# Sixty-five transposes of the identity in four of TensorE's waits, in a decoder of two layers on one core

## The chip, the cores and the metric

The kernel runs on one core of a Trainium2 chip. The core has five engines that run their own instruction streams and meet at semaphores: TensorE (matmuls and transposes; PE in the profile, its weight loads PEld), VectorE (DVE), ScalarE (ACT), GpSimd (POOL) and SyncE (SP, here used only to start transfers). TensorE reads from the on-chip memory and writes to eight accumulation banks; the other engines copy results out of these. The metric is the device time of one execution in microseconds, median over runs; lower is better.

## The reference

Two decoder layers in post-norm form over 16 sequences of 64 tokens with 128 features (1,024 tokens, eight tiles of 128). Each layer adds self-attention, cross-attention and a feed-forward part, with a layer norm behind each:

```
x = _layernorm(x + _L0_attn_ref(x, ...))
x = _layernorm(x + _L0_xattn_ref(x, ctx_1024, ctx_1024, mask, ...))
x = _layernorm(x + _L0_ffn_ref(x, gate_w, wg, wu, wd))
x = _layernorm(x + _L1_attn_ref(x, W_qkv, W_out))
x = _layernorm(x + _L1_xattn_ref(x, ctx_1024, ctx_1024, mask, ...))
x = _layernorm(x + _L1_ffn_ref(x, W_fc, ln_w, ln_b, W_proj))
```

The third line is a mixture of experts: a gate picks two of eight experts for each token, each expert computes `silu(x @ wg.T) * (x @ wu.T)` with 512 inner features and projects back with `wd`, and the two results are added with softmax weights. The fourth is self-attention with 16 heads of 64 features ("wide" in the kernel). The last has ternary weights: a matrix is divided by the mean of its magnitudes and rounded to -1, 0 or 1. All inputs and outputs are fp32.

## The kernel before

Each engine's instruction stream is written out by hand, in program order, with semaphore waits; no planner reorders anything. The kernel has three stages.

**First stage.** `stream_pe` and its four companions run the first two attentions as a software pipeline over 16 tiles. `drain_pe` ends it: beside the last tiles it computes the gate's logits, ranks the tokens by expert, and transposes the 24 expert weight matrices in four banks (L1347), each group copied back by ScalarE (L1352). GpSimd scatters the tokens' rows to a table in device memory, in the order of their experts (L1437).

**Experts** (`Routed`). The table is worked off in 23 blocks of 128 rows. For block j TensorE transposes its rows (`block_pe`, L1521, bank 6), ScalarE copies them out (L1527), TensorE does the gate and up projections (L1549, L1557; four matmuls each, which the profile shows as eight, since an fp32 matmul runs in two passes), ScalarE does the SiLU, VectorE the product, TensorE the down projection (L1580, bank 7). `Routed.pe` runs two blocks ahead with the transposes. Transposing block j+1 waits until ScalarE has copied block j out. Before block 0's copy ScalarE has two copies of weights for blocks 0 and 1 in its stream (`bring_act`, L1531); for later blocks GpSimd makes these copies (L1537).

**Bridge and second stage.** Behind the last block TensorE transposes weights of the next layers (L793, L270), multiplies the wide value weights with the output weights (L805), projects a bias (`fc.project_bias`, L985), and makes the column means of the ternary projection (`fc.means_pe`, L1004), for which it waits until VectorE has scaled the projection (L993). GpSimd gathers each token's two expert rows from the table (L1706): tiles 0 and 1, then tile 0's rsqrt (L1729), tile 2, tile 1's rsqrt, tiles 3 and 4, the rsqrt of tiles 2 and 3 (L1727, L1729), and so on in pairs. VectorE combines the rows of a tile (L1714, L1717), takes the statistics, and normalizes (`apply`, L1734). `turn_pe` (L1744) transposes the normalized tile for the next stage, and ScalarE copies it (L1750). Then `stream_pe` starts over with the wide attention: four projections of queries and keys per tile (`qkw_pe`, L831, 32 matmuls in the profile), scores (L858), value projections (L844). Their results go through three banks, 6, 7 and 4, in turn, and ScalarE and VectorE copy them out (L881). VectorE's row maxima are L403.

Bank 4 (`B_Y`) is not used from the end of the first stage to a matmul of two columns at block 8 (L949), and from there to the wide projections. `ident` is the 128 x 128 identity, loaded with the constants at the start.

Of the kernel before, what the change touches and what calls it, by code (L numbers as in the profile page):

```python
# [15 lines left out]
P = 128  # L16
# [62 lines left out]
def decoder_kernel(nc, A, out):  # L79
    with ExitStack() as ctx:  # L80
# [28 lines left out]
        PS = ctx.enter_context(nc.psum_tensor("banks", [P, 8, BANK], F32))  # L109

        B_S, B_PT, B_Y, B_OX, B_K, B_Q = 0, 2, 4, 5, 6, 7
# [74 lines left out]
        ident = cst[:, C_ID:C_ID + P]  # L186
# [65 lines left out]
        class Transposes:  # L252
# [7 lines left out]
            def pe(self, pe, some=None):  # L260
                for g in some or range(len(self.groups)):
                    waits, blocks, _ = self.groups[g]
                    for s, v in waits:
                        pe.wait_ge(s, v)
                    last = g - len(self.banks)
                    if last >= 0:
                        pe.wait_ge(self.copied[last % 2], last // 2 + 1)
                    bank = self.banks[g % len(self.banks)]
                    for n, (src, k) in enumerate(blocks):
                        m = pe.transpose(PS[:, bank, n * P:n * P + k], src, ident[0:k, 0:k])  # L270
                    m.then_inc(self.mm, 1)
# [72 lines left out]
        class Stage:  # L344
# [16 lines left out]
            def x_pe(self, pe, job):  # L361

                i = job.i
                pe.wait_ge(*self.norm.ln.at(i + 1))
                if i + 1 < NT:
                    pe.wait_ge(*self.norm.r.at(i + 2))
                elif job.after is not None and not self.wide and not job.after.stage.early:
                    pe.wait_ge(*job.after.stage.norm.r.at(1))
                if i >= 1:
                    pe.wait_ge(*self.norm.xev.at(i))  # L370
                pe.transpose(PS[:, B_OX, 2 * P:3 * P], X[:, i, :], ident).then_inc(self.norm.xmm.sem, 1)
# [49 lines left out]
            def t_pe(self, pe, job):  # L421

                i, n = job.i, job.n
                pe.wait_ge(*(self.share if self.wide else self.exp).at(i + 1))
                for m in range(2):
                    if job.before:
                        pe.wait_ge(*job.before.pt_read(m))
                    for r in range(4 * m, 4 * m + 4):
                        t = pe.transpose(PS[:, B_PT + m, P * (r % 4):P * (r % 4 + 1)], PR[:, n % 2, P * r:P * (r + 1)], ident)  # L429
                    t.then_inc(self.t_mm.sem, 1)  # L430
# [881 lines left out]
        class Routed:  # L1312
# [183 lines left out]
            def rows_sp(self, sp):  # L1496
# [14 lines left out]
                for j in range(BLOCKS):  # L1511
# [2 lines left out]
                    sp.wait_ge(*self.ycp.at(j + 1))  # L1514
                    sp.dma_start(routed[bass.ds(at[j], P), :], YS[:, j % 3, :]).then_inc(s_ys[j % 3], 16)

            def block_pe(self, pe, j):
                pe.wait_ge(s_xg[j % 4], 16 * (j // 4 + 1))
                if j >= 1:
                    pe.wait_ge(*self.xgt.at(j))  # L1520
                pe.transpose(PS[:, 6, 0:P], XG[:, j % 4, :], ident).then_inc(self.xt_mm.sem, 1)  # L1521
# [69 lines left out]
            def pe(self, pe):  # L1591
                last = pre[-1]
                pe.wait_ge(*last.y_read())
                pe.wait_ge(*self.rk.at(len(GROUPS)))
                pe.wait_ge(*self.map.at(8))
                _, e = nc.values_load_multi_w_load_instructions(
                    bi[0:1, 0, 0:BLOCKS], engines=[mybir.EngineType.PE], min_val=0, max_val=EXPERTS - 1,
                    skip_runtime_bounds_check_because="a sum of seven comparisons, each 0 or 1")
                pe.wait_ge(*self.w_cp.at(3 * EXPERTS))
                self.block_pe(pe, 0)  # L1600
                self.block_pe(pe, 1)
                for n in range(BLOCKS + 1):
                    if n + 2 < BLOCKS:
                        self.block_pe(pe, n + 2)
                    if n == 8:
                        fc.totals(pe, self.mul.at(n - 1))
                    if n < BLOCKS:
                        self.gate_pe(pe, n)
                    if n == 9:
                        pe.wait_ge(*fc.thr.at(2))  # L1610
                    if n < BLOCKS:
                        self.up_pe(pe, n)
                    if n >= 1:
                        self.down_pe(pe, n - 1, e[n - 1])
                pe.wait_ge(s_sep, 3)
                pe.wait_ge(*self.silu.at(BLOCKS))
                wide.weights_pe(pe)
                pe.wait_ge(*self.xgt.at(BLOCKS))
                fct.pe(pe, [0])
                pe.wait_ge(*self.ycp.at(BLOCKS))  # L1620
                fct.pe(pe, [1])
                pe.wait_ge(*self.mul.at(BLOCKS))
                wide.products_pe(pe)
                fc.project_bias(pe)
                fc.means_pe(pe)
                pe.wait_ge(*fc.bias.at(1))
                self.turn_pe(pe, (0,))

# [443 lines left out]
```

## Time and profile before

| | |
|---|---|
| median of three runs | 376.67 us |
| the runs | 373.87, 376.67, 377.61 us |
| profiled execution, first to last instruction | 377.6 us |
| TensorE busy | 336.8 us, 89% of the span |
| VectorE, ScalarE, GpSimd busy | 236.4, 183.6, 202.1 us |
| TensorE's mean granted clock | 0.964 of full speed |

The profiled execution's own time is its span, 377.6 us; it is the same as the highest run to the digit given. Busy time is the time in which an engine has an instruction of its own under way; TensorE's matmuls overlap one another, and their ends are modelled. The granted clock is the share of TensorE's full clock (2.4 GHz) that it was given; in this trace it has two levels, 1.00 and 0.50.

### The profile page before, as it was taken

What the parts mean: (1) busy time and instruction counts of PE and PEld (TensorE: products, weight loads), DVE (VectorE), ACT (ScalarE), POOL (GpSimd) and SP (SyncE); (2) the same over time, 40 slices, a digit from 0 to 9 for tenths busy, and PEclk for the clock granted to TensorE, in tenths of its full rate; (3) what the DMA queues carried; (4) which work ended last, traced back from release to release, by engine and by line L of the source; (5) the groups of instructions that cost most, each with busy time, mean ns of one, the idle gap of its engine ahead of it and who ended that gap; (6) DMA issues with size and microseconds to landing.
All of it is one profiled execution on the core that took longest, in us unless ns stands there. A gap on an engine that the chain in (4) does not pass through costs nothing.

```text
span 377.6 us, 9893 instructions
## 1 busy us (share of the span) xinstructions
PE 336.8 (89%) x3774; PEld 264.6 (70%) x3774; DVE 236.4 (63%) x561; ACT 183.6 (49%) x383; POOL 202.1 (54%) x287
## 2 busy tenths in 40 slices
PE   3879999998885589999997799889999999999994
PEld 2556677665774489999997675657788665676773
DVE  2798987778755013574335477746666577887585
ACT  2466776665653823233224134433544344776641
POOL 1856988885667124553413776322222057476785
PEclk9989999999989669999999699999999999999999
DMA  6799996000001101111101111000000000000001
GB/s 191 219 308 256 293 338 176 2 3 2 30 28 51 43 16 49 50 43 50 44 27 33 36 36 30 2 0 2 2 2 3 3 0 3 2 2 2 3 21 36
DMA packets 35993, 22.98 MB, mean 61 GB/s; under 512 B 4196, under 2 KB 33900, under 8 KB 35820
## 3 DMA queue, kind: packets, MB, share of 16 engines
q1 hardware_dynamic: 34636, 19.64, 17.9%
q0 software_dynamic: 1024, 2.10, 1.9%
q8 instruction: 31, 0.51, 0.5%
q10 hardware_dynamic: 288, 0.62, 0.5%
q14 instruction: 14, 0.11, 0.1%
HBM read 14.61 MB, written 7.73 MB: 59 GB/s over the span
## 4 chain that ended last, share of the span: by engine, by line
PE 76%; DVE 11%; issue 5%; ACT 3%; POOL 2%; DMA 1%; another core or an unknown queue 1%; SPq 0%; POOLq 0%; ACTq 0%; DVEq 0%
PE banks L429 7%; PE banks L844 7%; PE banks L831 6%; PE banks L1549 6%; PE banks L1557 6%; PE banks L539 6%; PE banks L566 6%; PE banks L1580 6%; PE banks L875 3%; PE banks L1347 3%; PE banks L511 3%; PE banks L523 2%; PE banks L1032 2%; PE banks L586 2%; PE banks L582 2%
## 5 line engine op out<-in xcount | busy, mean ns | idle before, releaser
L690 POOL TENSOR_TENSOR KB<-KT,cst 128x512 f32<-128x512 f32 x48 | 49.3, 1048 | 8.2 <-DVE KT L650 6.0
L403 DVE TENSOR_REDUCE mx<-banks 128x16 f32<-128x1024 f32 x32 | 38.6, 1207 | 13.5 <-PE banks L550 11.7
L438 ACT ACTIVATE PT<-banks 128x512 f32<-128x512 f32 x64 | 34.9, 595 | 23.6 <-PE banks L429 22.3
L1572 DVE TENSOR_TENSOR PT<-banks,PR 128x512 f32<-128x512 f32 x23 | 15.9, 691 | 47.9 <-PE banks L1557 43.7
L1537 POOL COPY U<-WALL 128x1024 f32 x21 | 21.9, 1043 | 42.6 <-PE banks L1557 35.9
L881 ACT ACTIVATE U<-banks 128x512 f32<-128x512 f32 x40 | 23.9, 597 | 38.1 <-PE banks L844 22.5
L331 POOL TENSOR_SCALAR ve<-mv 128x1 f32<-128x1 f32 x40 | 9.1, 229 | 54.0 <-DVE mv L326 53.6
L429 PE MATMUL banks<-cst,PR 128*128 128x128 f32 x256 | 35.6, 283 | 0.5 <-POOL PR L910 0.5
L419 ACT ACTIVATE PR<-PR 128x1024 f32<-128x1024 f32 x32 | 33.8, 1058 | 3.4 <-DVE PR L413 3.4
L831 PE MATMUL banks<-XT,WQKV 128*128 128x128 f32 x256 | 33.2, 292 | 0.4 <-ACT XT L1750 0.4
L844 PE MATMUL banks<-WALL,XT 128*64 128x512 f32 x128 | 29.7, 600 | 3.1 <-DVE U L881 2.8
L831 PEld LDWEIGHTS banks<-XT,WQKV 128*128 128x128 f32 x256 | 31.6, 205 | 1.1 <-ACT XT L1750 0.7
L429 PEld LDWEIGHTS banks<-cst,PR 128*128 128x128 f32 x256 | 28.3, 144 | 4.2 <-issue 2.0
L539 PE MATMUL banks<-KB,QS 64*64 64x512 f32 x192 | 27.8, 632 | 3.2 <-DVE PR L413 2.2
L413 DVE TENSOR_TENSOR PR<-banks,mx 128x1024 f32<-128x1024 f32 x24 | 29.4, 1225 | 0.8
L566 PE MATMUL banks<-VB,PT 128*64 128x18 f32 x768 | 26.7, 212 | 0.0
L566 PEld LDWEIGHTS banks<-VB,PT 128*64 128x64 f32 x768 | 24.3, 138 | 3.1 <-issue 0.3
L1549 PE MATMUL banks<-XGT,U 128*128 128x128 f32 x184 | 25.8, 286 | 0.0
L1557 PE MATMUL banks<-XGT,U 128*128 128x128 f32 x184 | 25.2, 281 | 0.0
L881 DVE COPY U<-banks 128x512 f32<-128x512 f32 x24 | 16.2, 687 | 14.2 <-PE banks L844 11.0
L1580 PE MATMUL banks<-WALL,PT 128*128 x184 | 24.4, 276 | 0.6 <-DVE YS L1588 0.6
L333 POOL TENSOR_TENSOR rstd<-ve,half 128x1 f32<-128x1 f32 x40 | 23.2, 579 | 3.3
(190 smaller groups left out, 699.5 us busy)
## 6 DMA issues: line engine op xcount, KB each, us to landing
routed_rows<-zero SPq DMA_DIRECT2D x1, 4544.0 KB, 19.1
WALL<-in_L_ffn_wg_dram SPq DMA_DIRECT2D x8, 256.0 KB, 5.0
WALL<-in_L_ffn_wu_dram SPq DMA_DIRECT2D x8, 256.0 KB, 5.3
WALL<-in_L_ffn_wd_dram SPq DMA_DIRECT2D x8, 256.0 KB, 5.7
U<-in_L_attn_W_qkv_dram SPq DMA_DIRECT2D x1, 1536.0 KB, 23.0
XG<-routed_rows SPq DMA_DIRECT2D x23, 64.0 KB, 1.8
routed_rows<-YS SPq DMA_DIRECT2D x23, 64.0 KB, 1.6
cst<-shape_constants ACTq DMA_DIRECT2D x1, 537.0 KB, 4.6
```

The lines of the kernel that those rows point to most:

```text
L403: dve.tensor_reduce(mx[:, n % 2, :], s, AX.X, ALU.max).then_inc(self.max.sem, 1)
L429: t = pe.transpose(PS[:, B_PT + m, P * (r % 4):P * (r % 4 + 1)], PR[:, n % 2, P * r:P * (r + 1)], ident)
L438: act.activation(PT[:, n % 2, 4 * m:4 * m + 4, :].rearrange("p r q -> p (r q)"), PS[:, B_PT + m, :], ACT.Copy).then_inc(self.pt.sem, 1)
L539: pe.matmul(PS[q, B_S + g, :], QS[f, n % 3, q], KB[f, n % 2, b].rearrange("p h k -> p (h k)"), start=True, stop=False)
L566: m = pe.matmul(PS[64 * b:64 * b + 64, B_Y, w * r:w * (r + 1)], PT[:, n % 2, r, 64 * b:64 * b + 64], VB[:, n % 3, r, b].rearrange("p a e - ...
L690: pool.tensor_tensor(KB[:, n % 2, b], bc(KT[:, n % 2, b, :], 1, 8), bc(cst[:, C_HEAD:C_HEAD + 8], 2, SEQ), ALU.mult).then_inc(self.kb.sem, 1)
L831: m = pe.matmul(PS[:, bank, P * k:P * (k + 1)], WQKV[:, f // 2, P * u:P * (u + 1)], XT[:, P * i:P * (i + 1)], start=True, stop=True)
L844: m = pe.matmul(PS[64 * a:64 * a + 64, bank, :], XT[:, SEQ * (2 * i + b):SEQ * (2 * i + b + 1)], WVO[:, a, 4 * g:4 * g + 4, :].rearrange(" ...
L881: return eng.activation(o, s, ACT.Copy) if part == 0 else eng.tensor_copy(o, s)
L1549: m = pe.matmul(PS[:, j % 2, P * c:P * (c + 1)], WE[:, j % 3, 0, P * c:P * (c + 1)], XGT[:, j % 3, :], start=True, stop=True)
L1557: m = pe.matmul(PS[:, 2 + j % 2, P * c:P * (c + 1)], WE[:, j % 3, 1, P * c:P * (c + 1)], XGT[:, j % 3, :], start=True, stop=True)
L1580: m = pe.matmul(PS[:, 7, 0:P], HT[:, j % 2, c, :], WALL[:, e, 2, P * c:P * (c + 1)], start=(c == 0), stop=(c == CH - 1))
```

## The change

A new function writes the transpose of the identity into the first 128 columns of bank 4, a given number of times. It has no wait, and its result is read by nobody. It is called at four places of `Routed.pe`: 27 times between the transposes of blocks 0 and 1, 6 times between those of blocks 1 and 2, 14 times between the projection of the bias and the column means, and 18 times between these and the turn of tile 0. Nothing else differs.

```
+            def turn_over(self, pe, n):
+
+                for _ in range(n):
+                    pe.transpose(PS[:, B_Y, 0:P], ident, ident)
...
                 self.block_pe(pe, 0)
+                self.turn_over(pe, 27)
                 self.block_pe(pe, 1)
+                self.turn_over(pe, 6)
                 for n in range(BLOCKS + 1):
                     if n + 2 < BLOCKS:
                         self.block_pe(pe, n + 2)
...
                 wide.products_pe(pe)
                 fc.project_bias(pe)
+                self.turn_over(pe, 14)
                 fc.means_pe(pe)
+                self.turn_over(pe, 18)
                 pe.wait_ge(*fc.bias.at(1))
                 self.turn_pe(pe, (0,))
```

## Rows read from the trace of the kernel before

**Rows 1.** The page: busy times, granted clock in 40 slices, chain by engine.

```profile
PE 336.8 (89%) x3774; PEld 264.6 (70%) x3774; DVE 236.4 (63%) x561; ACT 183.6 (49%) x383; POOL 202.1 (54%) x287
...
PEclk9989999999989669999999699999999999999999
...
PE 76%; DVE 11%; issue 5%; ACT 3%; POOL 2%; DMA 1%; another core or an unknown queue 1%; SPq 0%; POOLq 0%; ACTq 0%; DVEq 0%
```

**Rows 2.** Timeline at the first block: start, us, engine, line, operation, count [idle before <-releaser].

```profile
124.75 3.67 PE L1347 MATMUL banks<-cst,WALL 128*128 128x128 f32 x16 [0.31 <-ACT WALL L1352]
...
129.12 0.33 PE L1521 MATMUL banks<-cst,XG 128*128 128x128 f32 x1 [0.69 <-ACT WALL L1352]
...
130.48 1.99 ACT L1531 ACTIVATE U<-WALL 128x1024 f32 x2
...
132.78 0.45 PE L1521 MATMUL banks<-cst,XG 128*128 128x128 f32 x1 [3.33 <-ACT XGT L1527]
...
133.68 0.45 PE L1521 MATMUL banks<-cst,XG 128*128 128x128 f32 x1 [0.46 <-ACT XGT L1527]
...
139.90 1.06 PE L1580 MATMUL banks<-WALL,PT 128*128 x8
```

**Rows 3.** Stretches of 1 us there: busy us (instructions) by engine, clock, DMA share, GB/s.

```profile
121.00:122.00 1.00, 0.12 (x2) 0.00 (x0) 0.00 (x0) 0.00 (x0) 0.69 (x2) 0.82 0.12 41
...
128.00:129.00 1.00, 0.43 (x3) 0.03 (x1) 0.00 (x0) 0.75 (x2) 0.00 (x0) 0.76 0.00 0
...
131.00:132.00 1.00, 0.00 (x0) 0.00 (x0) 0.00 (x0) 1.00 (x2) 0.00 (x0) 0.94 0.00 0
...
138.00:139.00 1.00, 1.00 (x7) 1.00 (x7) 0.36 (x1) 0.09 (x1) 0.78 (x1) 0.64 0.00 0
```

**Rows 4.** Timeline at the first gathered tile, and tile 2's projections.

```profile
205.03 1.16 PE L985 MATMUL banks<-FCT,PT 128*128 128x128 f32 x8
...
207.93 1.16 PE L1004 MATMUL banks<-FCT,PT 128*128 128x128 f32 x8 [1.74 <-DVE FCT L993]
...
210.72 0.34 DVE L1734 TENSOR_SCALAR X<-R,mv,rstd 128x128 f32<-128x128 f32 x1 [1.01 <-POOL rstd L1729]
...
211.21 0.45 PE L1744 MATMUL banks<-cst,X 128*128 128x128 f32 x1 [2.12 <-DVE X L1734]
...
212.03 6.30 PE L831 MATMUL banks<-XT,WQKV 128*128 128x128 f32 x32 [0.37 <-ACT XT L1750]
...
218.36 0.69 DVE L881 COPY U<-banks 128x512 f32<-128x512 f32 x1 [3.18 <-PE banks L831]
...
229.39 3.84 PE L831 MATMUL banks<-XT,WQKV 128*128 128x128 f32 x32
```

**Rows 5.** Stretches of 1 us at the first gathered tile.

```profile
210.00:211.00 1.00, 0.00 (x0) 0.00 (x0) 0.28 (x2) 0.00 (x0) 0.73 (x3) 0.70 0.00 0
...
217.00:218.00 1.00, 1.00 (x10) 1.00 (x10) 0.00 (x0) 0.53 (x1) 0.90 (x1) 0.89 0.23 66
```

**Rows 6.** Timeline: transposes at full clock, in a row and alone.

```profile
116.42 1.95 PE L1347 MATMUL banks<-cst,WALL 128*128 128x128 f32 x16
...
143.59 0.27 PE L1521 MATMUL banks<-cst,XG 128*128 128x128 f32 x1
```

**Rows 7.** One stretch from the first down projection to the last block's end.

```profile
139.90:199.55 59.65, 59.65 (x535) 59.47 (x533) 27.52 (x53) 17.82 (x40) 24.46 (x22) 1.00 0.15 42
```

**Rows 8.** Timeline behind tile 0's projections.

```profile
218.35 0.94 POOL L1706 DMA_INDIRECT KB<-routed_rows,pos  x1 [0.30 <-issue]
...
220.34 0.25 POOL L1727 TENSOR_SCALAR ve<-mv 128x1 f32<-128x1 f32 x1 [1.04 <-DVE mv L1722]
...
222.78 1.21 DVE L403 TENSOR_REDUCE mx<-banks 128x16 f32<-128x1024 f32 x1
...
225.17 0.68 DVE L881 COPY U<-banks 128x512 f32<-128x512 f32 x1
...
225.90 0.36 PEld L844 LDWEIGHTS banks<-WALL,XT 128*64 128x64 f32 x4 [0.50 <-DVE U L881]
```

More of the change, by code:

```diff
@@ L1515, in rows_sp, with turn_over @@
                     sp.dma_start(routed[bass.ds(at[j], P), :], YS[:, j % 3, :]).then_inc(s_ys[j % 3], 16)
+            def turn_over(self, pe, n):
+                for _ in range(n):
+                    pe.transpose(PS[:, B_Y, 0:P], ident, ident)
             def block_pe(self, pe, j):
@@ L1600, in pe @@
                 self.block_pe(pe, 0)
+                self.turn_over(pe, 27)
                 self.block_pe(pe, 1)
+                self.turn_over(pe, 6)
                 for n in range(BLOCKS + 1):
@@ L1624, in pe @@
                 fc.project_bias(pe)
+                self.turn_over(pe, 14)
                 fc.means_pe(pe)
+                self.turn_over(pe, 18)
                 pe.wait_ge(*fc.bias.at(1))
```

## The prediction

> **What bounds the kernel now.** I read the page's top first: TensorE is busy in 89% of the span, and the chain that ended last lies on it for 76% [rows 1]. So the time is TensorE's, and what matters is how fast its clock runs and where it stands still. The page's clock line is 9 nearly everywhere; around the change it holds two low spots, a pair of sixes at 123 to 142 us and one six at 208 to 217 us [rows 1]. I then went through both in order of time, and through one-microsecond stretches for the granted clock (1.00 is the 2.4 GHz level, 0.50 the 1.2 GHz level).
>
> *First expert block* [rows 2, 3]. The last expert weights are transposed until 128.4 us. Block 0's transpose starts at 129.12 and lasts 0.33 us; the next one starts at 132.78, after 3.33 us of idle time that ends with ScalarE's copy of block 0, queued behind its two 1 us weight copies (L1531). The granted clock had come back to 1.00 at about 128.5 us (mean 0.76 in 128 to 129), falls at about 131.9 (0.94 in 131 to 132), and is back at about 138.7 (0.64 in 138 to 139). So blocks 0 and 1 run at half speed: from block 1's transpose at 132.78 to the first down projection at 139.90 pass 7.12 us.
>
> *First gathered tile* [rows 4, 5]. TensorE stands idle for 1.74 us in front of the means (L1004, 207.93) and for 2.12 us in front of tile 0's turn (L1744, 211.21). The clock falls at about 210.4 (0.70 in 210 to 211) and returns at about 217.2 (0.89 in 217 to 218). The 32 wide projections of tile 0 take 6.30 us; the same 32 take 3.84 us for tile 2, at 1.00 [rows 4].
>
> **The change, part by part.** It removes no wait and moves nothing. It adds 65 transposes, each with its weight load, all of the identity into bank 4. No engine waits for them and they wait for nothing; the only thing queued behind them is TensorE's own next step. The price of one: 16 transposes in a row at 1.00 take 1.95 us, with the last one's 0.27 us in it, so (1.95 - 0.27)/15 = 0.112 us each [rows 6]; 535 matmuls in 59.65 us give the same [rows 7]. At 0.50, 16 take 3.67 us with 0.45 in it: 0.215 us each [rows 2]. That the input is the identity on both sides the trace does not show; its bounds are these two prices, and I take 0.112, from the row whose clock applies at 129 us. Instruction feed is no limit: the same 59.65 us ran 535 matmuls and 533 loads without a gap [rows 7].
>
> *27 behind block 0.* They can start at 129.12 + 0.11 = 129.23 and take 27 x 0.112 = 3.02 us: over at 132.25, and block 1 starts at 132.78 anyway. Cost nothing, covered by ScalarE's two weight copies [rows 2]; without that cover they would cost their 3 us.
>
> *6 behind block 1.* From 132.89 they last to 132.89 + 0.67 = 133.56. Block 2 waits for ScalarE's copy of block 1. At full clock a lone transpose takes 0.27 instead of 0.45 us [rows 2, 6], so block 2 could start 0.18 sooner than 133.68, at 133.50. Cost 0.06.
>
> *What the first two buy.* If TensorE is busy from 129.12 on, there is no idle stretch for the clock to fall in. From block 2's transpose to the first down projection lie 1 + 8 + 8 + 1 + 8 + 8 = 34 matmuls (each projection of four fp32 matmuls shows as 8): 34 x 0.1115 = 3.79 us, so that projection starts at 133.56 + 3.79 = 137.35 instead of 139.90. **2.55 us** gained. All of it passes on: up to 199.55 TensorE is busy 59.65 of 59.65 us [rows 7], and the copies of weights on GpSimd and the loads on SyncE's queue wait for TensorE's steps, so they come earlier too. Bounds: nothing if the clock falls all the same, 2.6 if the six cost nothing.
>
> *14 and 18.* The 14 start at 205.03 + 8 x 0.112 = 205.93, end at 207.50 and have until 207.93; they lie under VectorE's scaling of the projection. The 18 start at 207.93 + 0.90 = 208.83, end at 210.85, and the turn starts at 211.21; they lie under the mixing and normalizing of tile 0 on VectorE and GpSimd, the last step of which is L1734 [rows 4]. Cost nothing, with 0.4 us to spare at either place; without the cover, 1.6 and 2.0 us.
>
> *What these buy.* With the clock at 1.00 the turn's transpose is 0.18 us shorter and the projections 6.30 - 3.84 = 2.46: VectorE's copy of the last projection moves from 218.36 to 215.72, 2.64 us sooner [rows 4]. But I don't book 2.64. Behind that copy VectorE combines tiles 2 and 3, GpSimd makes their rsqrt (L1727), and only then VectorE normalizes them and goes to the row maxima (L403) [rows 8]. GpSimd comes to that rsqrt only behind its gathers, which TensorE's clock does not move: the last starts at 218.35 and lasts 0.94, to 219.29. The rsqrt started at 220.34 after 1.04 us idle. It can start 1.04 us sooner and no more. The row maxima at 222.78, the copy at 225.17 and the projection's weight load at 225.90, which waited 0.50 us for exactly that copy, all follow. So **1.04 us** is gained and 1.6 are lost to the gathers: what is late next is GpSimd. Bounds: 0 (should the gathers' landing bind too; the trace shows no wait for one) and 2.64.
>
> **Sum.** 2.55 + 1.04 = 3.6 us. The profiled span of 377.6 is equal to the highest of the three runs (377.61), so I see nothing around it; 377.6 - 3.6 = 374.0. Against the median of 376.67 the same gain gives 373.1. The three runs lie 3.7 us apart, and one trace can't tell how much of that is low stretches being longer or shorter; those at the two places would go. I take the middle, **373.5**.
>
> **The skill against the trace.** 16 transposes in a row, with no other matmul among them, ran from 124.75 to 128.42, and the granted clock went from 0.50 to 1.00 at about 128.5 [rows 2, 3]. So transposes did bring the clock back here. The Trainium skill, "TensorE: Matmul & The Clock Gate", Part 4: PE-mode transpose, says the opposite: that the full clock does not engage for transposes because they don't count as busy in the same way. By that rule the filler would not hold the clock and the time would be that of rival (a), 1 to 2 us above before; by the rows it is the sum above. Trace and rule differ here, and I go by the trace.
>
> **Rivals.**
> *(a) The clock falls under the filler, and the change ends slower.* For it: no row has an operand that is the identity on both sides, nearly all zeros; and the clock also fell at 121.6 [rows 3], behind transposes with gaps between them. Against: the 16 transposes that brought it back [rows 2, 3]. Priced from rows: the 27 run at full clock until 131.9 (24 of them), the last 3 at 0.215, and end at 132.5, before 132.78. The 6 then take 1.29 us in 0.68 us of room (133.00 to 133.68): 0.6 late. The 18, if low from their first, take 3.87 us from 208.83 to 212.70: 1.5 late; if the clock falls at 210.4, 0.1. Nothing is gained: 377.6 + 0.7 to 2.1 = 378.3 to 379.7, or 377.4 to 378.8 from the median. It decides at one point: the granted clock in the microsecond before block 1. (The Trainium skill's rule on transposes, above, would lead here.)
> *(b) The filler meets a clock that is still low.* The clock came back only 0.6 us before block 0 [rows 2, 3]. If in most runs it comes back later, the 27 take 27 x 0.215 = 5.8 us, end at 135.03 and hold block 1 up by 2.25: of 2.55 some 0.3 stay, with the 1.04 behind: 376.3, or 375.3 from the median.
> *(c) GpSimd's gathers don't hold the second gain.* Then 2.55 + 2.64 = 5.2: 372.4, or 371.5 from the median. For it: later idle time of VectorE could give some back. Against: TensorE's load at 225.90 already waited for VectorE [rows 8].
>
> **How the numbers follow.** The forecast has 0.62, (a) 0.12, (b) 0.13, (c) 0.13. The forecast's own spread is 373.1 to 374.0 by the choice of base, and about 1 us more either way for the runs' spread. The range: down to (c)'s lower value, 371.5; up past (b) from the median, 376.0; outside lie (a), (b) from the profiled time and the ends. 1%, about what can be told from no change, is 3.8 us: faster means under 372.9. Nearly all of (c) lies there and some four tenths of the forecast: 0.13 x 0.9 + 0.62 x 0.4 = 0.37. Slower means over 380.4: only the upper end of (a) with the runs' spread on top, 0.04. The rest, 0.59, is within 1%.
>
> **What would show it.** Right: the clock at 1.00 from 129 to 206 us and on to the second tile; block 2 starting about 0.8 us after block 1; the first down projection 4.6 us after block 1's transpose (7.1 before); tile 0's 32 projections in 3.8 us; GpSimd's rsqrt of tile 2 without idle time in front of it, and TensorE's load for the third value projection waiting over a microsecond for VectorE's copy. Wrong: 0.50 anywhere behind the filler, block 1 or the turn starting later than the copy or normalizing step that it waits for, or row maxima more than 2 us earlier relative to the turn.

## The result, and the profile after

The changed kernel took 376.73 us (median of four runs, 375.49 to 378.6) against 375.27 for the kernel before in the same rounds (371.75 to 377.61): ratio 1.0133, with a 95% interval from 1.0075 to 1.0191. In later rounds, with 12 and 29 runs, it was 374.13 against 372.06: 1.0048, from 1.0011 to 1.0084. **The change makes the kernel slower, by 0.5 to 1.3%;** the forecast was 373.5, 0.8% faster than the median shown. The ratios leave each kernel's slowest runs out, so they need not be the ratio of the medians, which is 1.0039 here and 1.0056 in the later rounds.

The page after:

```profile
span 375.2 us, 10023 instructions
...
PE 341.6 (91%) x3839; PEld 270.2 (72%) x3839; DVE 236.3 (63%) x561; ACT 182.9 (49%) x383; POOL 201.6 (54%) x287
...
PEclk9989999999859899999999989999999999999998
...
PE 72%; DVE 13%; issue 5%; POOL 4%; DMA 3%; ACT 2%; SPq 1%; POOLq 0%; ACTq 0%; DVEq 0%
```

Answering to [rows 1]: TensorE has 4.8 us more busy time, the two low spots of the clock line are smaller, and the chain has lost some of TensorE's share (76 to 72%) to VectorE, GpSimd and DMA. A third low spot, 8 and 5 at 94 to 113 us, lies ahead of everything that the change touches. Two things mislead. This span of 375.2 belongs to a run of 377.04, so 1.8 us lie around a span; and the first trace's span was 2.4 us longer than this one although the kernel before is the faster one. Spans of single executions don't order these two kernels, and the traces show why: the clock ahead of the experts differs from one execution to the next, in code that no variant changes. The mean granted clock from 90 to 117 us, the number before the last two of a line, was 1.00 in the trace of experiment 4 and 0.62 in that of experiment 2:

```profile
90.00:117.00 27.00, 22.58 (x291) 19.13 (x291) 19.59 (x99) 17.87 (x41) 18.52 (x26) 1.00 0.10 33
90.00:117.00 27.00, 24.49 (x209) 20.79 (x209) 14.90 (x66) 12.16 (x29) 13.89 (x20) 0.62 0.06 20
```

In these two traces the last weight transpose (L1347) ends at 119.00 and 125.03 us, in all thirteen between 117.8 and 128.4. From that end to the end of the span the kernel before took 249.2 us (377.6 - 128.42, first trace) and 249.0 (370.0 - 120.97, experiment 3), the changed one 252.1 (375.2 - 123.10) and 252.2 (373.1 - 115.87 - 5.00, experiment 5). So in the stretch that the change can reach, both traces of the changed kernel are about 3 us slower, 0.8%. Below I compare distances within traces, from one step to another.

The timeline at the first expert block after. New line numbers: the filler is L1520, the blocks' transposes L1526, ScalarE's copies of them L1532, the down projection L1585.

```profile
118.10 5.00 PE L1347 MATMUL banks<-cst,WALL 128*128 128x128 f32 x44
...
127.44 0.45 PE L1526 MATMUL banks<-cst,XG 128*128 128x128 f32 x1 [4.34 <-DMA XG<-routed_rows]
...
127.68 4.60 PE L1520 MATMUL banks<-cst 128*128 128x128 f32 x27
127.92 0.28 ACT L1532 ACTIVATE XGT<-banks 128x128 f32<-128x128 f32 x1 [0.25 <-PE banks L1526]
...
132.12 0.27 PE L1526 MATMUL banks<-cst,XG 128*128 128x128 f32 x1
...
132.88 0.27 PE L1526 MATMUL banks<-cst,XG 128*128 128x128 f32 x1
...
136.73 1.06 PE L1585 MATMUL banks<-WALL,PT 128*128 x8
```

Answering to [rows 2]: TensorE now waits in front of block 0, 4.34 us for the load of its rows, and not behind it. ScalarE copies block 0 out at once, by 128.20. Block 1's transpose could follow then; it starts at 132.12, behind the 27. The prediction had named this as a sign of being wrong: block 1 later than the copy that it waits for.

The granted clock there, in stretches of 1 us (busy time of the engines, clock, DMA share, GB/s):

```profile
126.00:127.00 1.00, 0.00 (x0) 0.00 (x0) 0.00 (x0) 1.00 (x2) 0.00 (x0) 1.00 0.23 66
127.00:128.00 1.00, 0.56 (x3) 0.59 (x4) 0.00 (x0) 0.75 (x2) 0.00 (x0) 0.66 0.26 74
...
130.00:131.00 1.00, 1.00 (x8) 1.00 (x7) 0.00 (x0) 0.00 (x0) 0.00 (x0) 0.64 0.00 0
131.00:132.00 1.00, 1.00 (x11) 1.00 (x10) 0.00 (x0) 0.00 (x0) 0.00 (x0) 1.00 0.00 0
```

The clock falls at about 127.3, at the end of the wait for the load, and comes back at about 130.7, while TensorE does nothing but transposes of the identity. Of the 27, 15 start at 0.50.

The first gathered tile after (turn L1753, combining L1723, rsqrt L1736, gathers L1715):

```profile
207.68 0.30 PE L1753 MATMUL banks<-cst,X 128*128 128x128 f32 x1 [0.27 <-DVE X L1743]
...
208.35 3.84 PE L831 MATMUL banks<-XT,WQKV 128*128 128x128 f32 x32 [0.37 <-ACT XT L1759]
...
212.22 0.69 DVE L881 COPY U<-banks 128x512 f32<-128x512 f32 x1 [0.58 <-PE banks L831]
212.30 0.96 POOL L1715 DMA_INDIRECT KB<-routed_rows,pos  x1 [0.30 <-issue]
...
215.77 0.26 POOL L1736 TENSOR_SCALAR ve<-mv 128x1 f32<-128x1 f32 x1
...
216.71 0.35 DVE L1723 SCALAR_TENSOR_TENSOR R<-KB,pk,X 128x128 f32<-128x128 f32 x1 [2.60 <-DMA KB<-routed_rows,pos]
...
219.30 1.21 DVE L403 TENSOR_REDUCE mx<-banks 128x16 f32<-128x1024 f32 x1
...
222.42 3.27 PE L844 MATMUL banks<-WALL,XT 128*64 128x512 f32 x8 [2.56 <-DVE U L881]
```

Answering to [rows 4, 8]: the turn starts on time, the clock is at 1.00 there, the 32 projections take 3.84 us (6.30 before), and VectorE's copy comes 4.54 us behind the turn (7.15 before). GpSimd's rsqrt of tile 2 comes 8.09 us behind the turn, without idle time in front of it, where it came after 9.13: the 1.04 us that the prediction had booked. But VectorE then waits 2.60 us for tile 3's gathered rows, and the row maxima start 11.62 us behind the turn (11.57 before). TensorE waits for VectorE for 2.56 us, the clock falls again (below), and the value projections that follow take 3.27 us for eight matmuls, where eight behind tile 0's turn took 1.94.

```profile
222.00:223.00 1.00, 0.58 (x4) 0.28 (x6) 0.97 (x2) 0.00 (x0) 0.70 (x1) 0.94 0.25 66
223.00:224.00 1.00, 1.00 (x6) 0.39 (x4) 0.00 (x0) 0.00 (x0) 0.94 (x1) 0.50 0.29 66
```

### The profile page after: what moved, and what is told of

It is laid out like the page before. It is cut to its first block, busy times and chain, and to the rows that moved or that the text cites. A ratio compares the mean times of both kernels' runs of the same rounds, so it can differ in the third digit from the quotient of the medians.

```text
span 375.2 us, 10023 instructions
## 1 busy us (share of the span) xinstructions
PE 341.6 (91%) x3839; PEld 270.2 (72%) x3839; DVE 236.3 (63%) x561; ACT 182.9 (49%) x383; POOL 201.6 (54%) x287
## 4 chain that ended last, share of the span: by engine, by line
PE 72%; DVE 13%; issue 5%; POOL 4%; DMA 3%; ACT 2%; SPq 1%; POOLq 0%; ACTq 0%; DVEq 0%
PE banks L429 7%; PE banks L844 7%; PE banks L566 6%; PE banks L1585 6%; PE banks L1554 6%; PE banks L1562 5%; PE banks L539 5%; PE banks L831 4%; PE banks L875 3%; PE banks L511 2%; PE banks L523 2%; PE banks L1032 2%; PE banks L1347 2%; PE banks L586 2%; PE banks L582 2%
## 5 line engine op out<-in xcount | busy, mean ns | idle before, releaser
L844 PE MATMUL banks<-WALL,XT 128*64 128x512 f32 x128 | 31.2, 623 | 5.4 <-DVE U L881 5.1
L831 PE MATMUL banks<-XT,WQKV 128*128 128x128 f32 x256 | 30.7, 278 | 0.4 <-ACT XT L1759 0.4
L831 PEld LDWEIGHTS banks<-XT,WQKV 128*128 128x128 f32 x256 | 29.2, 192 | 1.0 <-ACT XT L1759 0.6
L1585 PE MATMUL banks<-WALL,PT 128*128 x184 | 24.4, 276 | 0.6 <-DVE YS L1593 0.6
L1715 POOL DMA_INDIRECT KB<-routed_rows,pos x16 | 15.8, 990 | 16.4 <-DMA routed_rows<-YS 12.3
L910 POOL TENSOR_TENSOR PR<-PR,rs 128x1024 f32<-128x1024 f32 x8 | 15.2, 1903 | 17.2 <-DVE rs L920 17.2
L1554 PE MATMUL banks<-XGT,U 128*128 128x128 f32 x184 | 24.4, 276 | 0.0
```

The lines of the kernel that those rows point to most:

```text
L831: m = pe.matmul(PS[:, bank, P * k:P * (k + 1)], WQKV[:, f // 2, P * u:P * (u + 1)], XT[:, P * i:P * (i + 1)], start=True, stop=True)
L844: m = pe.matmul(PS[64 * a:64 * a + 64, bank, :], XT[:, SEQ * (2 * i + b):SEQ * (2 * i + b + 1)], WVO[:, a, 4 * g:4 * g + 4, :].rearrange(" ...
L1554: m = pe.matmul(PS[:, j % 2, P * c:P * (c + 1)], WE[:, j % 3, 0, P * c:P * (c + 1)], XGT[:, j % 3, :], start=True, stop=True)
L1585: m = pe.matmul(PS[:, 7, 0:P], HT[:, j % 2, c, :], WALL[:, e, 2, P * c:P * (c + 1)], start=(c == 0), stop=(c == CH - 1))
```

## The experiments

Theory A: in most executions block 0 waits for its rows, ScalarE's weight copies are done by then, and the 27 have no cover. Theory B: the 27 and 6 work as predicted and the loss is in the second stage.

**1. The 27 and the 6 alone.** From the changed kernel:

```
                 fc.project_bias(pe)
-                self.turn_over(pe, 14)
                 fc.means_pe(pe)
-                self.turn_over(pe, 18)
```

> Only the 27 and the 6 at the first expert block; the 14 and 18 are left out. Theory A (in most executions block 0's rows come late and ScalarE's two weight copies are long done when they come, so the 27 have no cover and stand in the path: 27 x 0.112 = 3.0 us at full clock, 27 x 0.215 = 5.8 at half, less the 0.7 us that block 1 waits for the copy of block 0 anyway): slower than before by 1 to 3 us. Theory B (the first block's filler does what was predicted, and the loss is in the second stage, where the gathers' landing holds VectorE and TensorE's clock falls a few us later): faster than before by 1 to 2.5 us.

Measured: 374.62 against 371.8, ratio 1.0101 (1.0049 to 1.0152). As theory A says. The 27 and 6 alone make the kernel slower. In its trace the 27 take 4.59 us, and block 1 starts 4.67 us behind block 0, as in the changed kernel.

**2. The 14 and the 18 alone.** The calls with 27 and 6 taken out.

> Only the 14 and the 18 in front of the first gathered tile; the 27 and 6 are left out. Theory A: within 1 us of before. In its trace the clock is 1.00 at the turn, tile 0's projections take 3.8 us, and the row maxima start 11.6 us after the turn, as before, since the combining of tile 3 waits for its gathered rows. Theory B: slower than before by 1 to 3 us, with a low stretch of the clock at the value projections that before does not have.

Measured: 370.64 against 371.8, ratio 0.9974 (0.992 to 1.0028): no difference, against theory B. With nothing behind block 0, block 1 follows it after 0.90 us. Its row maxima started 10.20 us behind the turn, a little sooner than I expected of A.

**3. The kernel before, once more.** No edit.

> The kernel before, unchanged, for a second trace of it. Both theories: same time within 0.5%. Theory A: in its trace block 1's transpose starts about 0.8 us after block 0's, which itself waited for the load of its rows; the 3.66 us of the first trace was one execution's, in which ScalarE stood still for 3.1 us on something outside the core's own engines. Theory B: 3 to 4 us from block 0 to block 1 again.

Measured: 371.81 against 371.8, ratio 1.0012 (0.9968 to 1.0057). Its timeline at the first block:

```profile
span 370.0 us, 9893 instructions
...
115.97 5.00 PE L1347 MATMUL banks<-cst,WALL 128*128 128x128 f32 x44
...
123.56 1.98 ACT L1531 ACTIVATE U<-WALL 128x1024 f32 x2
...
125.44 0.45 PE L1521 MATMUL banks<-cst,XG 128*128 128x128 f32 x1 [4.47 <-DMA XG<-routed_rows]
...
126.34 0.45 PE L1521 MATMUL banks<-cst,XG 128*128 128x128 f32 x1 [0.46 <-ACT XGT L1527]
...
132.96 1.06 PE L1580 MATMUL banks<-WALL,PT 128*128 x8
```

Block 0 waits 4.47 us for its rows, ScalarE's weight copies are over at 125.54, and block 1 follows after 0.90 us, not 3.66. The first trace was the odd one, and it said so, in rows of ScalarE and of SyncE's loads that the prediction does not use:

```profile
122.67 0.60 ACT L1352 ACTIVATE WALL<-banks 128x512 f32<-128x512 f32 x1 [2.26 <-remote]
...
124.10 3.25 ACT L1352 ACTIVATE WALL<-banks 128x512 f32<-128x512 f32 x6 [0.83 <-remote]
```

```profile
124.05 10.58 SPq L1507 DMA_DIRECT2D XG<-routed_rows  x7
```

ScalarE stood still for 3.1 us on something outside the core's engines (the profile says only "remote"); in none of the twelve later traces does it wait so in this stretch. That held the last weight copies back. Block 0's rows were asked for at 124.05. The loads land in 1.8 us by the page's median, so by estimate these were there at about 125.9, 3 us ahead of block 0's transpose at 129.12.

**4. 27 in front of block 0, no other filler.**

```
+                self.turn_over(pe, 27)
                 self.block_pe(pe, 0)
```

> 27 transposes in front of block 0's transpose instead of behind it; no other filler. Theory A: they lie in the wait for block 0's rows (4.3 us in the trace of the changed kernel), cost nothing, and hold the clock: 0 to 2.5 us faster than before, and 1 to 4 us faster than the 27 and 6 behind block 0. Theory B: TensorE's wait for ScalarE's copies is behind block 0, so 27 in front cost up to 3 us: slower than before by 0 to 3 us.

Measured: 370.08 against 371.8, ratio 0.9949 (0.9895 to 1.0002): 0.5% faster, at the edge of what the runs can tell.

```profile
120.76 3.14 PE L1520 MATMUL banks<-cst 128*128 128x128 f32 x27 [1.76 <-ACT WALL L1352]
123.74 0.27 PE L1526 MATMUL banks<-cst,XG 128*128 128x128 f32 x1
124.47 0.30 PE L1526 MATMUL banks<-cst,XG 128*128 128x128 f32 x1 [0.46 <-ACT XGT L1532]
...
129.11 1.06 PE L1585 MATMUL banks<-WALL,PT 128*128 x8
```

The same 27 in the wait that is really there: block 1 starts 0.73 us behind block 0, and the first down projection 5.37 us behind block 0 (7.52 in experiment 3, 9.29 in the changed kernel).

**5. The changed kernel, once more.** No edit.

> The changed kernel, unchanged, on one chip with the three below and for a second trace. Theory A (27 and 6 behind block 0 are in the path; 14 and 18 gain little, since the gathers bind): slower than before by 1 to 4 us; block 1 starts 3.6 to 4.7 us behind block 0. In the second stage the row maxima start 10.2 to 11.6 us behind the turn, bound by gathered rows or by GpSimd. Theory B' (the 4.67 us from block 0 to block 1 were one execution's): same time as before, block 1 within 1 us of block 0.

Measured: 374.13 against 372.06, ratio 1.0048 (1.0011 to 1.0084).

```profile
span 373.1 us, 10023 instructions
...
115.87 5.00 PE L1347 MATMUL banks<-cst,WALL 128*128 128x128 f32 x44
...
125.48 0.45 PE L1526 MATMUL banks<-cst,XG 128*128 128x128 f32 x1 [4.61 <-DMA XG<-routed_rows]
125.72 5.84 PE L1520 MATMUL banks<-cst 128*128 128x128 f32 x27
...
131.39 0.27 PE L1526 MATMUL banks<-cst,XG 128*128 128x128 f32 x1
...
136.00 1.06 PE L1585 MATMUL banks<-WALL,PT 128*128 x8
```

Here the clock was low for all 27: block 1 came 5.91 us behind block 0. The row maxima started 11.49 us behind the turn, and VectorE waited 2.47 us for tile 3's rows.

**6. 54 instead of 27 behind block 0**, with the 6, without 14 and 18.

> 54 instead of 27 behind block 0, then the 6; the 14 and 18 are left out. Theory A: 27 more at 0.112 us each, 3.0 us slower than the kernel with 27 and 6 alone (which was 1.0101 of before), so 1.015 to 1.022 of before. Theory B' (covered work): within 1 us of the kernel with 27 and 6 alone.

Measured: 381.0 against 372.06, ratio 1.0233 (1.0155 to 1.0311); 1.3% more than with 27, some 5 us, where A expected 3.0 at full clock.

```profile
122.32 0.30 PE L1526 MATMUL banks<-cst,XG 128*128 128x128 f32 x1 [4.55 <-DMA XG<-routed_rows]
122.45 7.72 PE L1520 MATMUL banks<-cst 128*128 128x128 f32 x54
130.01 0.27 PE L1526 MATMUL banks<-cst,XG 128*128 128x128 f32 x1
```

54 held block 1 up to 7.69 us behind block 0, 3.0 more than the 4.67 of experiment 1's trace. That is A's price per transpose. The ratio's excess over it is within the two intervals, and its six runs spread from 373.72 to 381.61.

**7. 27 in front of block 0, and the 14 and 18.**

> 27 in front of block 0 instead of behind it, none behind block 1, and the 14 and 18 as in the change. Theory A: the gains of both add up, 2 us (1 to 4) faster than before. Theory C (what 27 ahead gain at the experts, the 14 and 18 lose again in the second stage, where TensorE then waits for VectorE and its clock falls later): no faster than the 27 ahead alone, which were 0.9949 of before.

Measured: 372.23 against 372.06, ratio 0.9963 (0.9913 to 1.0013); one of its twelve runs took 813.09 us, for a reason that no trace shows. As theory C says: no faster than experiment 4. C's reason does not show in its trace, though: the clock stays at 1.00 from 112 to 371 us.

**8. 36 in front of block 0, no other filler.**

> 36 instead of 27 in front of block 0, no other filler. The wait there was 4.3 to 4.6 us in four traces; 36 take 4.0. Theory A: no slower than with 27, and the clock holds through block 0 in more executions: 0 to 1 us faster than 27 ahead, 1 to 4 us faster than before. Against it: if the load of block 0's rows comes earlier in other executions, 36 stand in the path by up to 1 us.

Measured: 369.91 against 372.06, ratio 0.9947 (0.9909 to 0.9985). **The one kernel of the study whose interval lies below 1;** no better than 27. In its trace the 36 ended at 131.0 and block 0 came behind them at 130.85 without a wait: they were about 1 us too many, as the expectation feared.

**9. 36 earlier, in front of the wait for the last weight copy.**

```
                 pe.wait_ge(*last.y_read())
+                self.turn_over(pe, 36)
```

> 36 transposes right behind the last weight transposes, in front of the wait for the last weight copy (with 27 or 36 behind that wait, 1.7 us of the wait stayed idle and the 36 ended about 1 us after block 0's rows had landed); no other filler. Theory A: 36 x 0.112 = 4.0 us lie inside the 4.3 to 4.6 us that TensorE waits there; they cost nothing and the clock stays at 1.00 through the first blocks: block 1 within 0.8 us of block 0, first down projection 5.4 us behind block 0 (7.5 before); 1.5 to 3 us faster than before (0.992 to 0.996). Against it: the clock would have been at 1.00 there in most executions anyway: within 1 us of before.

Measured: 371.98 against 371.65, ratio 0.9994 (0.9946 to 1.0042): nothing gained, against the expectation.

```profile
125.83 4.09 PE L1520 MATMUL banks<-cst 128*128 128x128 f32 x36
...
130.52 0.30 PE L1526 MATMUL banks<-cst,XG 128*128 128x128 f32 x1 [0.59 <-DMA XG<-routed_rows]
```

```profile
132.00:133.00 1.00, 0.96 (x8) 0.99 (x8) 0.00 (x0) 0.28 (x1) 0.00 (x0) 0.90 0.35 104
```

They cost no time, but they end 0.6 us before block 0, the first three blocks come with 0.5 us waits between them, and the clock fell at about 132.8 all the same (0.90 in 132 to 133, 0.50 behind it). It need not fall: experiments 10 and 11 have the same 36 in the same place, and in their traces it holds at 1.00 there, with the first down projection 5.51 and 5.41 us behind block 0 (7.03 here). The ratios of experiments 8 and 9 have overlapping intervals, so that experiment 8's kernel does better is not shown.

**10. 36 early, and each pair's rsqrt ahead of the next gather on GpSimd.**

```
                     self.gather(pool, t + 1)
                     if t + 2 < NT:
-                        self.gather(pool, t + 2)
                         self.rsqrt(pool, t)
                         self.rsqrt(pool, t + 1)
+                        self.gather(pool, t + 2)
```

> As the kernel with 36 early, and on GpSimd each pair's rsqrt comes ahead of the gather of the tile behind it (tile 4's gather behind the rsqrt of tiles 2 and 3, and so on). If GpSimd's order sets the row maxima (the step of the prediction): 0 to 1 us faster than with 36 early alone. If the landing of tile 3's rows sets them: no difference, and in its trace the rsqrt of tile 2 comes long before that of tile 3.

Measured: 371.85 against 371.65, ratio 0.999 (0.9945 to 1.0036). No difference in time, though in its trace the clock holds at the first block:

```profile
129.57 0.30 PE L1526 MATMUL banks<-cst,XG 128*128 128x128 f32 x1 [0.57 <-DMA XG<-routed_rows]
...
135.08 1.06 PE L1585 MATMUL banks<-WALL,PT 128*128 x8
```

The 2 to 2.5 us saved there against experiments 3 and 2 would be 0.5 to 0.7%, at or past the edge of the interval; whether the gain is smaller in most executions or lost elsewhere is not shown.

**11. As 10, with the 14 and 18.**

> As the one with 36 early and gathers later, and the 14 and 18 in front of the first gathered tile. If GpSimd's order held their gain back: the row maxima start 8.5 to 9.5 us behind the turn (10.2 to 11.6 in four traces with the 14 and 18) and the kernel is 1 to 2.5 us faster than without them. If the landing of tile 3's rows holds it back: 10.2 to 11.6 us again, no faster than without them; VectorE waits for a DMA in front of tile 3's combining.

Measured: 374.82 against 371.65, six runs, five of them from 374.32 to 376.07 and one of 368.21; there is no ratio, and its time settles nothing. Its trace does (gathers L1714, rsqrt L1735, combining L1722, turn at 206.71):

```profile
211.33 0.96 POOL L1714 DMA_INDIRECT KB<-routed_rows,pos  x1 [0.30 <-issue]
...
213.22 0.23 POOL L1735 TENSOR_SCALAR ve<-mv 128x1 f32<-128x1 f32 x1 [0.94 <-DVE mv L1730]
...
215.62 0.35 DVE L1722 SCALAR_TENSOR_TENSOR R<-KB,pk,X 128x128 f32<-128x128 f32 x1 [2.48 <-DMA KB<-routed_rows,pos]
...
218.22 1.21 DVE L403 TENSOR_REDUCE mx<-banks 128x16 f32<-128x1024 f32 x1
```

With no gather in its way GpSimd made tile 2's rsqrt 6.51 us behind the turn (9.13 in the first trace). The row maxima started 11.51 us behind the turn all the same: VectorE waited 2.48 us for tile 3's rows. The landing of that gather holds them, not GpSimd's order.

## Why the prediction was wrong

**The step that failed: "27 behind block 0. Cost nothing, covered by ScalarE's two weight copies".** The cover was in the one trace I had and in no later one; what is there instead is a wait of 4.3 to 4.6 us for block 0's rows, in front of block 0. I priced its loss ("without that cover they would cost their 3 us") and gave that no rival and no chance. From block 0 to block 1 the kernel before needs 0.90 us (experiment 3), the changed kernel 4.68 and 5.91, with 54 it is 7.69. Rival (b) had the price of slow filler, 27 x 0.215 = 5.8 (measured: 5.84 in experiment 5), but set it against the same cover of 3.5 us. Its condition, a clock that is low when the filler starts, held in both traces of the changed kernel.

**The gain of 2.55 us.** Its size was right, its mechanism only in part. From block 1's transpose to the first down projection pass 4.61 us in both traces of the changed kernel (4.6 predicted; 7.12 and 6.62 before). But the prediction had the 27 hold the clock at 1.00. In the traces the clock had fallen already, in the wait in front of block 0 (at 127.3 and 124.5), and the 27 brought it back, at half speed for 15 and for all of them. That it was back before block 1, by 1.4 and by 0.1 us, was luck. That all of it passes on was right: from the first down projection to the end of the last one pass 61.4 us in all thirteen traces. Set against the filler's cost, block 0 to the down projection went from 7.52 and 8.02 (experiments 3 and 2) to 9.29 and 10.52 us: 1.3 to 3.0 us lost. Experiment 1's ratio, 1.0101 of 371.8, is 3.8 us (1.8 to 5.7). Experiments 4 and 8 show what the clock is worth where its filler is free: 5.37 us instead of 7.5 to 8.0, and about 0.5% of the time, with an interval below 1 in experiment 8 alone.

**The clock under the filler, rival (a).** Refuted: the clock rose from 0.50 to 1.00 while TensorE ran transposes of the identity alone, and in the five traces with the 14 and 18 it is at 1.00 under them. The Trainium skill, "TensorE: Matmul & The Clock Gate", Part 4: PE-mode transpose, has it that transposes don't count as busy in the same way; this trace differs again, at 130.7 us.

**14 and 18.** Their cost of nothing was right: TensorE still stands idle for 0.27 us in front of the turn, until VectorE has normalized the tile. Of their gain I had booked 1.04 of 2.64 and held that the gathers' issue on GpSimd takes the rest. GpSimd's step did come 1.04 us sooner, but it was not what VectorE waited for. The bound I set aside, 0, "should the gathers' landing bind too", is what happened in the changed kernel: row maxima 11.62 and 11.49 us behind the turn, 11.57 and 11.46 before. In experiments 2 and 7 the rows landed sooner (10.20 and 10.44), and without this filler, but with the clock falling later, it was 10.58 and 10.53 (experiments 1 and 4). So with the 14 and 18 the landing decides, it varies, and they are worth nothing that can be measured: 0.9974 (0.992 to 1.0028). They can even cost: in the changed kernel's first trace and in experiment 11 TensorE's wait for VectorE behind the row maxima ended in a fall of the clock (at 222.9 and 222.4). From the turn to the end that first trace took 167.5 us, against 166.4 and 166.1 before; the second trace of the changed kernel, without such a fall, took 166.1. So of the 3 us lost, up to half lay in the second stage in one trace and none in the other.

**The base.** I took the span of 377.6 for a run of 377.61, "nothing around it". With 1.8 us around a span that execution took about 379.4, longer than every run of the kernel before that was shown: a sign that this execution was not a usual one. The three runs were high as well: in the later rounds the kernel before had medians of 371.65 to 372.06, so the forecast of 373.5 is a gain only against these three.

**Open:** how large the loss is within 0.5 to 1.3%. The two intervals overlap (from 1.0075 to 1.0084), the first rounds have four runs of each kernel, and the traces say 0.8%, so the two ratios need not differ. The filler's own length varied between traces (4.60 and 5.84 us) with the clock, which would move the loss; it was not tried. What sets the clock's low stretch ahead of the experts, the largest difference between executions, is open too.

## What to carry to other kernels

Before work is put into an idle stretch, check that the stretch is there in more than one execution: look at what ended it, and at whether the step behind it could have started earlier (here the rows had landed 3 us before). A stall with a releaser outside the core's engines, or a span longer than the timed runs, can mark an odd execution. At the first block the 27 cost nothing in front of the step that waits for a load, as long as they ended before the load did, and gained some 0.5% at most; behind that step, with the next one ready after 0.9 us, nearly all of their time delayed the next step. Where executions differ ahead of the change by more than the change is worth, distances within traces, from a step that the change cannot reach, tell more than spans.

## What the runs showed of the hardware

The granted clock rose from 0.50 to 1.00 while TensorE ran nothing but transposes of the identity into a bank that nobody reads (at 130.7 and 131.3 us in the two traces of the changed kernel), as it did behind transposes of weights in the kernel before (at 128.5 us). A gather of 128 rows landed 1.7 to 3.5 us after its issue had ended (tile 3's, by VectorE's wait, in the five traces with the 14 and 18: 1.7 in experiment 2, 3.45 in the changed kernel's first trace), so a schedule that just fits it does not fit it every time. In unchanged code ahead of the experts the mean clock from 90 to 117 us was anything from 0.56 to 1.00 in these traces.
